# Second batch's output projections spread over feed-forward tiles 3 to 13, tile input centred and rounded on GpSimd

## The reference

```
x = x + attention(layernorm(x))          # 32 heads of 16, softmax, output weight w_o
x = x + ffn(layernorm(x))

ffn(x):
  beta  = mean(|x|);  xq = clip(round(x*sqrt7/(beta+eps)), -8, 7) * beta
  gate, up = xq @ ternary(w_gate), xq @ ternary(w_up)     # inner width 1376
  inter = up * relu(gate)^2
  gamma = max(|inter|); iq = clip(round(inter*127/(gamma+eps)), -128, 127) * gamma/127
  return iq @ ternary(w_down)
```

## Time and profile before

| | before |
|---|---|
| median of 3 runs | 977.27 us (976.27 to 977.34) |
| the profiled execution | 976.0 us |
| its span | 974.2 us |
| PE busy | 922.3 us, 95% |
| DVE busy | 834.5 us, 86% |
| ACT busy | 766.0 us, 79% |
| POOL busy | 157.4 us, 16% |
| feed-forward part | about 797 us to the end |

### The profile page before, as it was taken

The page is one execution under the profiler, slowest core; times in us unless marked ns, Lnnn a source line. Parts: engine busy times, 40 slices in busy tenths (PEclk is TensorE's granted clock), DMA queues, the critical chain, the costliest instruction groups (busy, mean ns, idle before and its releaser), DMA issues.

```text
span 974.2 us, 16581 instructions
## 1 busy us (share of the span) xinstructions
PE 922.3 (95%) x5806; PEld 287.9 (30%) x5806; DVE 834.5 (86%) x1516; ACT 766.0 (79%) x1480; POOL 157.4 (16%) x298
## 2 busy tenths in 40 slices
PE   4799899999999999999999999999999988899997
PEld 3333222222222222222222222222222224444443
DVE  6588799999999999999999999999992237878874
ACT  4343688888888988999899999899786557766665
POOL 3502011121111211111321111310012210112100
PEclk9999999999999999999999999999999999999999
DMA  8340021021121112412112510213540004411000
GB/s 303 94 153 1 12 62 40 24 55 51 50 55 39 40 34 75 149 37 56 39 52 58 154 46 24 56 55 104 142 125 12 12 11 142 129 44 44 32 24 33
DMA packets 38041, 64.90 MB, mean 67 GB/s; under 512 B 3654, under 2 KB 19014, under 8 KB 37702
## 3 DMA queue, kind: packets, MB, share of 16 engines
q1 hardware_dynamic: 37958, 63.85, 22.2%
HBM read 42.27 MB, written 21.23 MB: 65 GB/s over the span
## 4 chain that ended last, share of the span: by engine, by line
PE 79%; DVE 8%; ACT 7%; issue 3%; DMA 2%; SPq 1%; POOL 0%; ACTq 0%; POOLq 0%; DVEq 0%
PE ps L462 25%; PE ps L445 14%; PE ps L400 14%; PE ps L378 9%; PE ps L606 6%; DVE mx L1057 5%; PE ps L337 4%; PE ps L654 3%; PE ps L630 3%; ACT PB L816 2%; ACT PB L895 1%; ACT XV L873 1%; PE ps L427 1%; DMA tu<-wkT 1%; DVE XV L1151 1%
## 5 line engine op out<-in xcount | busy, mean ns | idle before, releaser
L1057 DVE TENSOR_REDUCE mx<-ps 128x1 f32<-128x512 f32 x1024 | 634.9, 683 | 33.8 <-PE ps L400 26.9
L816 ACT ACTIVATE PB<-ps 128x512 f32<-128x512 f32 x1024 | 539.6, 600 | 84.9 <-PE ps L445 83.9
L400 PE MATMUL ps<-QK 48*128 48x512 f16 x1024 | 304.6, 385 | 10.9 <-issue 5.3
L445 PE MATMUL ps<-QK 50*128 50x512 f16 x1024 | 301.1, 384 | 6.8 <-ACT PB L816 3.7
L462 PE MATMUL ps<-PB,Vg 128*32 128x512 f32 x2048 | 274.5, 608 | 1.9 <-ACT PB L816 0.6
L400 PEld LDWEIGHTS ps<-QK 48*128 48x128 f16 x1024 | 78.8, 93 | 203.5 <-DVE mx L1057 171.6
L445 PEld LDWEIGHTS ps<-QK 50*128 50x128 f16 x1024 | 74.7, 93 | 188.7 <-ACT PB L816 138.1
L378 PE MATMUL ps<-XV,wqk 128*128 128x512 f16 x384 | 110.7, 384 | 1.1 <-DVE wmean L994 1.1
L1293 POOL TENSOR_SCALAR nmb<-nm 128x16 f16<-128x16 f32 x32 | 6.6, 205 | 518.7 <-DVE nm L1062 518.7
L606 PE MATMUL ps<-wo,XV 128*128 128x512 f32 x128 | 61.0, 609 | 0.0
L462 PEld LDWEIGHTS ps<-PB,Vg 128*32 128x32 f32 x2048 | 40.4, 108 | 68.2 <-issue 43.3
(11 more groups left out here) (135 smaller groups left out, 671.0 us busy)
## 6 DMA issues: line engine op xcount, KB each, us to landing
parts_d<-spl SPq DMA_DIRECT2D x64, 128.0 KB
att_d<-OS SPq DMA_DIRECT2D x32, 256.0 KB
QK<-parts_d SPq DMA_DIRECT2D x48, 128.0 KB, 4.7
QK<-parts_d SPq DMA_DIRECT2D x16, 256.0 KB, 4.4
XV<-att_d SPq DMA_DIRECT2D x2, 2048.0 KB, 8.4
QK<-rden_d SPq DMA_DIRECT2D x8, 512.0 KB, 7.3
wqk<-x SPq DMA_DIRECT2D x16, 256.0 KB, 3.7
out<-PB SPq DMA_DIRECT2D x16, 256.0 KB, 2.0
```

The costliest lines, as they stand in the source:

```text
L400: nc.tensor.matmul(ps[:, at % S_BANKS, :], QK[rows, sup % 2, 2 * set_ + p, 0, half * HALF + qt * P:half * HALF + (qt + 1) * P], QK[rows, s ...
L445: nc.tensor.matmul(ps[:, tile_bank_of(place), :], QK[rows, sup % 2, 2 * set_ + p, 1, kt * P:(kt + 1) * P], QK[rows, sup % 2, 2 * set_ + p, ...
L816: nc.scalar.activation(PB[:, at % 3, i, :], ps[:, tile_bank_of(tile_place(sup * 4 + step // KEYT, step % KEYT, i)), :], ACT.Exp, scale=exp ...
L1057: nc.vector.tensor_reduce(mx[:, v % 2, idx, kh:kh + 1], ps[:, at % S_BANKS, :], AX.X, ALU.max).then_inc(s_used, 1)
```

## The change

The output projections of the second batch, tiles 8 to 15, take place in the tiles that the table `OUT_AT` gives (3, 4, 6, 7, 9, 10, 12, 13) instead of in each of 6 to 13, and `dve_x2` goes with them. The centring of a tile's input and its rounding move from DVE to POOL: POOL computes the negated mean `fneg` beside the reciprocal root, `pool_centre` adds it (x times one plus `fneg`), and `pool_quant` multiplies by the scale and adds the large constant. DVE keeps the clamp, now `dve_clamp`, which follows the multiply and reduce of the tile's first chunk. The reciprocal of the second batch's sums moves from p = 2 to p = 1. POOL's list for the feed-forward part is written out anew: in each tile the rounding of p+1, then, where `OUT_AT` has p, `pool_rstd` of the projected tile, then the centring of p+2, then the attention products.

```diff
--- before.py
+++ after.py
@@ -72,6 +72,7 @@
 WCOL = KT * INTER
 DCOL = IT * HID
 XRING = 8
+OUT_AT = {3: 8, 4: 9, 6: 10, 7: 11, 9: 12, 10: 13, 12: 14, 13: 15}
 TAIL = 16
 
 
@@ -146,6 +147,7 @@
         hm = sb("hm", [P, 2, 4], F32)
         fbag = sb("fbag", [P, TILES, 2], F32)
         frstd = sb("frstd", [P, TILES], F32)
+        fneg = sb("fneg", [P, TILES], F32)
 
 
         def xin(t):
@@ -241,6 +243,7 @@
         xr_in = [sem(f"xr_in{r}") for r in range(XRING)]
         att_ready, o_psum, x2_ready, f_stats = sem("att_ready"), sem("o_psum"), sem("x2_ready"), sem("f_stats")
         f_bn, f_var, f_rs, xh_ready, x_abs = sem("f_bn"), sem("f_var"), sem("f_rs"), sem("xh_ready"), sem("x_abs")
+        q_mag, f_neg = sem("q_mag"), sem("f_neg")
         q_step, xq_ready, xq_psum, xq_copy = sem("q_step"), sem("xq_ready"), sem("xq_psum"), sem("xq_copy")
         g_psum, u_psum, rel_ready, sq_ready = sem("g_psum"), sem("u_psum"), sem("rel_ready"), sem("sq_ready")
         h_ready, hm_step, hs_ready, y_ready = sem("h_ready"), sem("hm_step"), sem("hs_ready"), sem("y_ready")
@@ -721,8 +724,8 @@
                     pe_gate_up(pe, p, 2)
                 if tile_at(p + 1):
                     pe_xq_transpose(pe, p + 1)
-                if p + 2 >= BT and tile_at(p + 2):
-                    pe_attention_out(pe, p + 2)
+                if p in OUT_AT:
+                    pe_attention_out(pe, OUT_AT[p])
                 if tile_at(p - 1):
                     pe_down(pe, p - 1)
 
@@ -1091,8 +1094,8 @@
                 if t == 1:
                     for w in range(3):
                         dve.wait_ge(w_tern[w], PIECES if w else 4)
-                    dve_centre(dve, 0)
-                    dve_centre(dve, 1)
+                if t in (5, 6):
+                    dve_clamp(dve, t - 5)
                 if t in (4, 5):
                     dve_quant(dve, t - 4)
 
@@ -1111,16 +1114,9 @@
             dve.wait_ge(f_bn, t + 1)
             nc.vector.bn_aggr(fbag[:, t, :], bst[:, r, :]).then_inc(f_stats, 1)
 
-        def dve_centre(dve, t):
-
-            dve.wait_ge(f_stats, t + 1)
-            if t >= 2:
-                dve.wait_ge(xq_psum, t - 1)
-            nc.vector.tensor_scalar(xh[:, t % 2, :], xr[:, t % XRING, :], fbag[:, t, 0:1], None, ALU.subtract).then_inc(xh_ready, 1)
-
         def dve_quant(dve, t):
 
-            s, r, n = t % 2, t % 4, 4 * t
+            s, r, n = t % 2, t % 4, 3 * t
             mean = bsum[:, r:r + 1]
             dve.wait_ge(x_abs, t + 1)
             dve.wait_ge(f_rs, t + 1)
@@ -1134,9 +1130,11 @@
             dve.wait_ge(q_step, n + 2)
             nc.vector.tensor_scalar(bq[:, s, 2:3], bq[:, s, 1:2], frstd[:, t:t + 1], SQRT7, ALU.mult, ALU.mult)\
                 .then_inc(q_step, 1)
-            dve.wait_ge(q_step, n + 3)
-            nc.vector.tensor_scalar(xh[:, s, :], xh[:, s, :], bq[:, s, 2:3], MAGIC16, ALU.mult, ALU.add).then_inc(q_step, 1)
-            dve.wait_ge(q_step, n + 4)
+
+        def dve_clamp(dve, t):
+
+            s = t % 2
+            dve.wait_ge(q_mag, t + 1)
             nc.vector.tensor_scalar(xh[:, s, :], xh[:, s, :], MAGIC16 + 7.0, MAGIC16 - 8.0, ALU.min, ALU.max)\
                 .then_inc(xq_ready, 1)
 
@@ -1255,16 +1253,16 @@
                     dve_out(dve, p - 2)
                 if p >= 1 and tile_at(p + 1):
                     dve_quant(dve, p + 1)
-                if p == 2:
+                if p == 1:
                     dve_reciprocal(dve, 1)
                 if tile_at(p):
                     for c in range(NCH):
                         dve_inner(dve, p, c)
+                        if c == 0 and p >= 1 and tile_at(p + 1):
+                            dve_clamp(dve, p + 1)
                     dve_inner_scale(dve, p)
-                if tile_at(p + 2):
-                    if p + 2 >= BT:
-                        dve_x2(dve, p + 2)
-                    dve_centre(dve, p + 2)
+                if p in OUT_AT:
+                    dve_x2(dve, OUT_AT[p])
 
         def cast(out_, in_):
 
@@ -1362,9 +1360,24 @@
 
             r = t % 4
             own_wait(pool, f_stats, t + 1)
+            nc.gpsimd.tensor_scalar(fneg[:, t:t + 1], fbag[:, t, 0:1], -1.0, 0.0, ALU.mult, ALU.add).then_inc(f_neg, 1)
             nc.gpsimd.tensor_scalar(vpe[:, r:r + 1], fbag[:, t, 1:2], LN_EPS, 1.0, ALU.add, ALU.mult).then_inc(f_var, 1)
             own_wait(pool, f_var, t + 1)
             nc.gpsimd.tensor_tensor(frstd[:, t:t + 1], vpe[:, r:r + 1], expo[:, r:r + 1], ALU.pow).then_inc(f_rs, 1)
+
+        def pool_centre(pool, t):
+
+            own_wait(pool, f_neg, t + 1)
+            if t >= 2:
+                own_wait(pool, xq_psum, t - 1)
+            nc.gpsimd.tensor_scalar(xh[:, t % 2, :], xr[:, t % XRING, :], ones[:, 0:1], fneg[:, t:t + 1], ALU.mult, ALU.add)\
+                .then_inc(xh_ready, 1)
+
+        def pool_quant(pool, t):
+
+            own_wait(pool, q_step, 3 * t + 3)
+            nc.gpsimd.tensor_scalar(xh[:, t % 2, :], xh[:, t % 2, :], bq[:, t % 2, 2:3], MAGIC16, ALU.mult, ALU.add)\
+                .then_inc(q_mag, 1)
 
         @block.gpsimd
         def _(pool):
@@ -1423,10 +1436,25 @@
             for sup in range(SUPERS):
                 pool_superunit(pool, sup, sup // SPB, sup % SPB, (sup + 1) // SPB, (sup + 1) % SPB, sup == SUPERS - 1)
 
-            for t in range(TILES):
+            for t in range(BT):
                 pool_rstd(pool, t)
-                if t + 2 < TILES:
+                if t in (0, 1):
+                    pool_centre(pool, t)
+                if t + 2 < BT:
                     pool_att(pool, t + 2)
+                if t in (4, 5):
+                    pool_quant(pool, t - 4)
+            for p in range(TILES):
+                if p >= 1 and tile_at(p + 1):
+                    pool_quant(pool, p + 1)
+                if p in OUT_AT:
+                    pool_rstd(pool, OUT_AT[p])
+                if tile_at(p + 2):
+                    pool_centre(pool, p + 2)
+                if p in (2, 3):
+                    pool_att(pool, BT + p - 2)
+                if p in OUT_AT and OUT_AT[p] + 2 < TILES:
+                    pool_att(pool, OUT_AT[p] + 2)
 
 
         def sp_parts_out(sp, n):
```

## The result

The changed kernel takes 982.85 us (median of 4 runs, 981.58 to 983.99) beside 977.22 for the kernel before on the same chip: ratio 1.0062, interval 1.005 to 1.0074. It is slower by 5.6 us, where 4.65 were forecast. The profiled execution's span is 979.8 us against 974.2, the same 5.6.

A forecast was written before the change was run, and what follows sets the result against it. PE was busy 95% of the span; in tiles without a projection, ACT's list plus DVE's last two microseconds set the pace. +4.81 - 0.50 + 0.34 = +4.65 on the 977.27 median gave 981.9 us, range 977.5 to 986.5.

The forecast's parts named there:

- The new wait: GpSimd's centring behind projection statistics in eight tiles: first relu 1.06 us late, 0.50 swallowed; +4.81 over tiles 3 to 14.
- Moving the projections: Second batch's projections spread over other feed-forward tiles: dearer entries and cheaper exits cancel; 0, ends -2.4 and +2.4.
- The relief of DVE: Centring and rounding leave DVE, about 0.97 us per tile; worth 0 in tiles without projection, as the third multiply awaits ACT.
- The exit: After tile 14's first relu, the 0.50 us of PE's waits isn't met again: -0.50.
- The reciprocal: Second batch's reciprocal moves from tile 2 to tile 1: net +0.34, ends 0 and +1.5; needed for denominators in time.
- The shared port: A GpSimd product can hold DVE's scale for a whole operation; 0.15 us to spare before the first multiply, taken as 0.
- The sum: Whole kernel: +4.81 - 0.50 + 0.34 = +4.65 us, giving 981.9 us.
- Rival (a): No cost: ACT's 0.50 us of slack swallows the late centring in projection tiles; 977.6 us, chance 0.07.
- Rival (b): Faster: spread works as a queue filling PE's idle in tiles without projection, 2.0 us less; 975.6 us, chance 0.08.
- Rival (c): GpSimd's fp32 pass takes 1.27 us, as a product does; 5.0 us more, 986.9 us, chance 0.07.

The follow-up runs named there:

- centring first: Changed kernel with GpSimd's centring put before the wait for the projection's statistics in six of eight projection tiles; 976.44 us, ratio 1.0005.
- GpSimd alone: Changed kernel with projections back in tiles 6 to 13, reciprocal back in tile 2, GpSimd's first two products in tiles 4 and 5; 981.62 us, ratio 1.0052.
- spread alone: Kernel before with the second batch's projections spread and the reciprocal in tile 1, centring and rounding left on DVE; 977.15 us, ratio 1.001.
- centring before power: Changed kernel with GpSimd's centring between the negated mean and the variance and power, in all eight projection tiles; 976.21 us, ratio 0.9994.
- reciprocal in tile 2: Changed kernel with only the reciprocal of the second batch's sums put back in tile 2; 988.54 us, ratio 1.012.
- absolutes on DVE: ACT's mean of absolutes for tiles 2 to 15 moved to DVE; on the changed kernel 970.69 us, ratio 0.9941.
- kernel before with the absolutes on DVE: Kernel before with the mean of absolutes of tiles 2 to 15 moved from ACT to DVE, nothing moved to GpSimd; 975.24 us, ratio 0.9978.

## Why the prediction was right

**The new wait** was the step that decided, and it held: eight tiles whose centring stands behind the projection's statistics in GpSimd's list. Ordering alone removes it (centring first), GpSimd alone brings 5.0 of the 5.6 us (1.0052). The term was mis-sized a little: 12.27 us a tile forecast, 12.41 measured. Of the chain of 4.30 us, 4.45 are there: the centring takes 0.76 instead of 0.65, and from the negated mean to the next operation it is 0.28 instead of 0.19; the other links are within 0.04. Eight times 0.14 is 1.1 us. Tile 9 took 12.71, and its extra 0.30 lies in one pause on GpSimd: between the variance and the power it was idle for 0.47 us instead of 0.18.

```profile
905.10 0.54 POOL L1366 TENSOR_TENSOR frstd<-vpe,expo 128x1 f32<-128x1 f32 x1 [0.47 <-POOL vpe L1364]
```

Tile 12 took 12.49, since PE finished its projection 0.08 late. Why these two happened is open. Together they make the 1.5 us between 125.22 and 126.72.

**Moving the projections** was taken at 0; alone it gives 120.36 us relu to relu against 120.41, ratio 1.001 (this run has the earlier reciprocal as well).

**The relief of DVE** was taken at 0, and in the change it is: the tile without a projection stays at 9.02 us, though two DVE passes of 0.97 us together have left it.

**The exit**, -0.50, is -0.52.

**The reciprocal** was taken at +0.34 and is inside -0.15 with everything else of tiles 0 to 3. With centring and rounding left on DVE (spread alone) these tiles took 28.06 us against 27.69, +0.37. Its use was right: the denominators let the first product start at 823.98 (823.8 forecast), and without the move the kernel needs 988.5 us. Expected before that run were 988.

**The shared port** was taken at 0: DVE's scale at 851.77 was held to 0.34 us only, since it began late in the product. Where it was held longer (1.34 us at 850.76 in centring before power) the kernel still lost nothing that can be measured.

**The sum.** 4.65 is 1.0 us short of 5.64 because two misses partly cancel: +1.5 in tiles 3 to 14 and -0.5 in tiles 0 to 3. That it came so near owes something to this. The forecast's own range, 979.8 to 984.5, is also a little wider than its parts: 1.2 us either way and the reciprocal's ends give 980.4 to 984.3.

Rival (a) failed because the relu came 1.21 us later than before (4.45 against 3.24), of which ACT's slack took 0.5; the tile grew by the other 0.7. Rival (b) failed since ACT's list sets the tile without a projection. Its gain appeared only when that list was shortened: then relu to relu is 118.45 us. Rival (c) had the wrong size: 0.76 us, not 1.27.

Not settled: whether a centring that is late by less than the slack costs anything at all (centring before power has 120.85 us relu to relu, 0.5 more than the spread alone, and no loss that can be measured).

## What to carry to other kernels

Moving a pass to an idle engine moves it into that engine's order: ask what it will stand behind there, and what stands behind its consumer. Before relieving an engine, look, in each kind of tile, for the list that sets the pace; in the tiles without a projection that was ACT's. What one short pass taken from it brought depended on the rest: 0.2% in the kernel before (0.9978), 0.4% with the spread (0.9957), 0.6% with the whole change (0.9941).

## What the runs showed of the hardware

PE's clock fell in tile 1 in some profiles and not in others. Windows of two kernels, each from the first relu of tile 1 on: GpSimd alone, then reciprocal in tile 2. Through tile 1 the two have the same lists.

```profile
807.42:811.42 4.00, 2.06 (x18) 0.96 (x15) 3.26 (x9) 3.94 (x9) 1.45 (x2) 1.00 0.59 246
811.42:815.42 4.00, 3.95 (x14) 1.66 (x15) 2.30 (x8) 2.37 (x4) 0.00 (x0) 0.57 0.00 0
```

```profile
809.10:813.10 4.00, 2.05 (x18) 0.96 (x15) 3.26 (x9) 3.94 (x9) 1.44 (x2) 1.00 0.57 238
813.10:817.10 4.00, 3.95 (x22) 1.96 (x23) 2.98 (x9) 2.36 (x4) 0.00 (x0) 1.00 0.00 0
```

In the first PE worked 2.06 of 4 us and was then granted 0.57 of its clock as a mean over the next 4, so for most of them the level of 1.2 GHz. In the second it worked 2.05 and stayed at 1.00, the level of 2.4 GHz. So what PE did in these 4 us does not settle by itself whether the clock falls; what else does is open. In windows cut the same way, the clock fell in six other profiles, with 1.29 to 2.18 us of work in the first 4 (the kernel before and the changed one 2.06 each), and stayed at 1.00 in four of the five profiles with the absolutes on DVE, with 2.49 or 2.50 (the fifth, with everything else on DVE too, is among the six). Executions of one kernel differ too: the kernel before with the absolutes on DVE took 972.3 and 972.4 us with a mean clock of 0.992 and 0.993, and 974.1 to 976.1 with 0.988 to 0.991.

In the first of the two kernels above the down product of tile 0 falls into the low stretch and takes 4.23 us, in the second 2.54. Of these 1.7 us little is left at tile 3's first relu: tiles 0 to 3 took 27.47 and 27.00 us.

A pass of 128x512 in fp32 on GpSimd took 0.69 us with one scale from a column and a constant, 0.76 with two columns. The nearest form in the kernel before, with fp16 out, took 0.62 in the median and 0.67 in the mean.
